# A relational graph layer: ScalarE fetches 27 chunks of source rows instead of 23, ahead of normalising raw rows, and SyncE fetches one chunk more

## The chip, the cores and the metric

The kernel runs on one core of a Trainium2 chip. The metric is device time in microseconds (us). Before the change three runs gave 2043.67 us in the median (2040.7 to 2045.21). Engines are called PE (matrix products), DVE (VectorE), ACT (ScalarE), POOL (GpSimd) and SP (SyncE).

## The reference, cut to what matters

```python
# N = 12500 nodes, D = 256; 212500 edges sorted by dst; 8 relations
h   = relu(layernorm(x))                       # [N, D]
hx  = einsum('ni,rio->rno', h, weight)         # per relation
agg = segment_sum(hx[edge_type, src], dst, N)  # over the edges
out = x + agg*sqrt(0.5) + h_bias + (h @ loop_weight)*sqrt(0.5)
```

The kernel turns the order round: for each node and relation it first sums the rows of h over the edges, and then multiplies these sums by the relation's weights.

## The kernel before

**First phase, to about 115 us.** All rows of x are normalised and written to `h_table` in DRAM, 1 KB a row: 256 fp16 values and 256 fp16 remainders. Meanwhile POOL gathers the first 96 "raw" chunks from x itself, since these need no table.

**Main loop.** The edges are cut into 1661 chunks of 128. A step s (98 of them) takes 17 chunks, k = 0 to 16 (the last step has 12). A chunk needs its 128 source rows in SBUF, one row for each partition. They come in four ways:

- the last chunk (k = 16) of steps 0 to 95 is raw and was gathered in the first phase; it is normalised later, 8 chunks at a time (`scale_raw`, L477): for group g DVE takes the statistics at k = 1 to 8 of step 8g-4 and then works out the scales behind k = 9 (`scales`, L622), for which it waits for ACT's square root (`deviation`, L441; DVE waits on `s_std` at L626); ACT then scales the rows;
- 36 chunks (k = 8 of steps 3, 6, 8, 11, 14, 16, ...) are fetched by SP, row by row, into three buffers (L315 to L327): registers are loaded with 32 row offsets at a time (L321), then 32 DMAs of 1 KB follow (L326);
- 23 chunks (k = 4 of steps 7, 11, 15, ...) are fetched by ACT in the same manner, 32 rows in each of its iterations (L509 to L520), into two buffers;
- the other 1506 chunks are gathered by POOL, one indirect DMA each (L400), into 15 buffers. Before every fourth gather it waits until the chunk 12 gathers back has been summed (L398).

PE multiplies the chunk's rows with a one-hot matrix (L991; L973 for raw chunks) into one of six PSUM banks, and before the end of each chunk it waits until DVE has added the chunk five back (L959). DVE adds the result into a ring of sums in SBUF (L787) and makes the one-hot matrix of the chunk one step on (L726). From k = 5 on PE also does the fp32 products of the tile two steps back (L921, then L926), 18 of them, spread over the chunks left in the step. After the last chunk come the products of the last two tiles (L914).

**ACT's iteration t** (L559 to L570) runs beside step t+2: it stores the result of tile t-1 once DVE has it (DVE does so behind k = 1), clears a ring slot, copies the transposed own rows, issues two loads, normalises a raw group in every eighth iteration, and fetches 32 rows. Every engine runs its own instructions in order, and waits are semaphores written by hand.

Of the kernel before, what the change touches and what calls it, by code (L numbers as in the profile page):

```python
# [4 lines left out]
def relational_graph_layer(nc, x, src, dst, etype, weight, h_bias, loop_weight, out, edge_chunks):  # L5
# [8 lines left out]
    P = 128  # L14
    N, D = x.shape
    R = weight.shape[0]
    C = dst.shape[1]
    E_CHUNKS = edge_chunks
    TILES = -(-N // P)
    STEPS = TILES  # L20
    K = C // STEPS
# [8 lines left out]
    NB = 15  # L30
    SB = 3
    AB = 2
# [18 lines left out]
    SYNC_K = K // 2  # L51
    SYNC_STEPS = [range(3, STEPS - 1, 8), range(6, STEPS - 1, 8), range(8, STEPS - 1, 8)]
    SCALAR_K = 4
    SCALAR_STEPS = range(7, STEPS - 1, 4)
    SCALAR_ROWS = [(0, 32), (32, 64), (64, 96), (96, 128)]
    SYNC_LOAD = 32
    ROW_BYTES = 4 * D

# [15 lines left out]
    table_bytes = table.rearrange("n d -> (n d)").bitcast(mybir.dt.uint8).rearrange("(a b) -> a b", a=1)  # L74

    sync_steps = sorted(s for steps in SYNC_STEPS for s in steps)
    sync_chunks = [K * s + SYNC_K for s in sync_steps]
    list_ranges = [(K * steps[0] + SYNC_K, K * steps.step, len(steps)) for steps in SYNC_STEPS]
    scalar_chunks = [K * s + SCALAR_K for s in SCALAR_STEPS]
    list_ranges.append((K * SCALAR_STEPS[0] + SCALAR_K, K * SCALAR_STEPS.step, len(SCALAR_STEPS)))  # L80
    listed = [a + d * i for a, d, n in list_ranges for i in range(n)]
    LISTED = len(listed)

# [1 line left out]
    with ctx:  # L85
        def sb(name, shape, dt):
            return ctx.enter_context(nc.sbuf_tensor(name, shape, dt))
# [4 lines left out]
        def sem(name):  # L92
            return ctx.enter_context(nc.semaphore(name))
# [21 lines left out]
        rows = sb("rows", [P, NB + SB + AB, 2 * D], fp16)  # L115
        list_low = sb("list_low", [P, LISTED], i32)
        list_parts = sb("list_parts", [P, 2, LISTED], fp16)
        row_offsets = sb("row_offsets", [LISTED, P], i32)
# [100 lines left out]
        scalar_landed = [sem(f"scalar_rows_landed{b}") for b in range(AB)]  # L219
# [4 lines left out]
        summed = sem("chunk_summed")  # L224
# [56 lines left out]
        def raw_step(s):  # L281
            if s == 0:
                return 0
            g = (s + 4) // G
            return g if (s + 4) % G == 0 and 0 < g < RAW_GROUPS else None
# [5 lines left out]
        def _(sp):  # L291
# [23 lines left out]
            def fetch_rows(j):  # L315
                b = j % SB
                if j >= SB:
                    sp.wait_ge(summed, sync_chunks[j - SB] + 1)
                q = listed.index(sync_chunks[j])
                for p in range(0, P, SYNC_LOAD):  # L320
                    _, start = nc.values_load_multi_w_load_instructions(  # L321
                        row_offsets[q:q + 1, p:p + SYNC_LOAD], engines=[mybir.EngineType.SP],
                        min_val=0, max_val=(N - 1) * ROW_BYTES,
                        skip_runtime_bounds_check_because="the sources of edges are nodes")
                    for i in range(SYNC_LOAD):
                        sp.dma_start(rows[p + i:p + i + 1, NB + b, :].bitcast(mybir.dt.uint8),  # L326
                                     table_bytes[:, bass.ds(start[i], ROW_BYTES)]).then_inc(sync_landed[b], 16)  # L327
# [112 lines left out]
        def _(act):  # L440
# [15 lines left out]
            for i in range(LN_GROUPS + 1):  # L456
                n, g = group_rows(i)
                b = i % 2
# [18 lines left out]
            def scale_raw(g):  # L477
                i = LN_GROUPS + 1 + g
                deviation(i)
                act.wait_ge(s_scale, i + 1)  # L480
                act.wait_ge(s_raw[g], 16 * G)
                for j in range(G):
                    last = nc.scalar.activation(raw[:, G * g + j, :], raw[:, G * g + j, :], ACT.Relu,  # L483
                                                bias=shift[:, i % 2, j:j + 1], scale=rstd[:, i % 2, j:j + 1])
                last.then_inc(s_norm, 1)

            def clear_tile(t):
                act.wait_ge(out_ready, t + 1)
                nc.scalar.copy(ring[:, :, ring_slot(t):ring_slot(t) + P],  # L489
                               zeros[:, :].unsqueeze(1).broadcast_to([P, HR, P])).then_inc(cleared, 1)  # L490

            def own_tile(t):
                n = P if t < TILES - 1 else LAST
                if t >= 2:
                    act.wait_ge(hT_ready, t - 1)
                act.dma_start(own[0:n, t % 2, :], table[t * P:t * P + n, :]).then_inc(own_landed[t % 2], 16)

            def own_x_tile(t):
                n = P if t < TILES - 1 else LAST
                if t >= 2:  # L500
                    act.wait_ge(scaled, t - 1)
                act.dma_start(own_x[0:n, t % 2, :], x[t * P:t * P + n, :]).then_inc(x_landed[t % 2], 16)

            def store_tile(t):
                n = P if t < TILES - 1 else LAST
                act.wait_ge(result_ready, t + 1)
                act.dma_start(out[t * P:t * P + n, :], result[0:n, t % 2, :]).then_inc(stored[t % 2], 16)

            def fetch_rows(t):  # L509
                j, (a, b) = t // len(SCALAR_ROWS), SCALAR_ROWS[t % len(SCALAR_ROWS)]  # L510
                if a == 0 and j >= AB:
                    act.wait_ge(summed, scalar_chunks[j - AB] + 1)
                q = listed.index(scalar_chunks[j])
                _, start = nc.values_load_multi_w_load_instructions(
                    row_offsets[q:q + 1, a:b], engines=[mybir.EngineType.Activation],
                    min_val=0, max_val=(N - 1) * ROW_BYTES,
                    skip_runtime_bounds_check_because="the sources of edges are nodes")
                for p in range(a, b):
                    act.dma_start(rows[p:p + 1, NB + SB + j % AB, :].bitcast(mybir.dt.uint8),
                                  table_bytes[:, bass.ds(start[p - a], ROW_BYTES)]).then_inc(scalar_landed[j % AB], 16)  # L520

            def copy_hT(t, to=own_hT):
                act.wait_ge(hT_ready, t + 1)
                nc.scalar.copy(to[:, :, :], ps_hT[:, 0:D].rearrange("p (h n) -> p h n", h=H)  # L524
                               ).then_inc(hT_copied, 1)
# [21 lines left out]
            with act.If(unfit < 1):  # L547
                for b in range(2):
                    act.wait_ge(s_tab[b], TAB_DONE[b])
                act.wait_ge(s_split, LN_GROUPS + 1)  # L550
                for a, b in ((0, 2 * P), (2 * P, SPAN)):
                    nc.scalar.copy(ring[:, :, a:b], zeros[:, 0:1].unsqueeze(1).broadcast_to([P, HR, b - a])
                                   ).then_inc(s_zeros, 1)
                for t in range(2):
                    own_tile(t)
                own_x_tile(0)
                scale_raw(0)
                act.wait_ge(list_ready, 1)
                for t in range(TILES - 2):  # L559
                    if t >= 1:  # L560
                        store_tile(t - 1)
                        if t <= TILES - RING + 1:
                            clear_tile(t - 1)
                    copy_hT(t)
                    own_tile(t + 2)
                    own_x_tile(t + 1)
                    if raw_step(t + 2) is not None:
                        scale_raw(raw_step(t + 2))
                    if t < len(SCALAR_ROWS) * len(scalar_chunks):
                        fetch_rows(t)  # L570
                for i in range(2):
                    copy_hT(TILES - 2 + i, last_hT[i])
                store_tile(TILES - 3)
                own_x_tile(TILES - 1)
                for i in range(2):
                    store_tile(TILES - 2 + i)
# [517 lines left out]
```

## Time and profile before

| | |
|---|---|
| median of three runs | 2043.67 us |
| the profiled execution's own time | 2044.47 us |
| its span | 2042.7 us |
| POOL busy | 1522.1 us, 75% |
| PE busy | 1529.7 us, 75% |
| DVE busy | 1335.0 us, 65% |
| ACT busy | 342.8 us, 17% |
| 16 DMA engines, share in the main loop | 0.46 |
| granted TensorE clock, mean | 0.878 |

The busy figures don't count instructions that issue DMAs or load registers. ACT's 17% is therefore its arithmetic alone, and SP, which only issues, has no busy time at all. For these two the time between rows is what counts.

### The profile page before, as it was taken

What the parts mean: (1) busy time and instruction counts of PE and PEld (TensorE: products, weight loads), DVE (VectorE), ACT (ScalarE), POOL (GpSimd) and SP (SyncE); (2) the same over time, 40 slices, a digit from 0 to 9 for tenths busy, and PEclk for the clock granted to TensorE, in tenths of its full rate; (3) what the DMA queues carried; (4) which work ended last, traced back from release to release, by engine and by line L of the source; (5) the groups of instructions that cost most, each with busy time, mean ns of one, the idle gap of its engine ahead of it and who ended that gap; (6) DMA issues with size and microseconds to landing.
All of it is one profiled execution on the core that took longest, in us unless ns stands there. A gap on an engine that the chain in (4) does not pass through costs nothing.

```text
span 2042.7 us, 45665 instructions
## 1 busy us (share of the span) xinstructions
PE 1529.7 (75%) x10568; PEld 1179.3 (58%) x10568; DVE 1335.0 (65%) x4141; ACT 342.8 (17%) x427; POOL 1522.1 (75%) x1610
## 2 busy tenths in 40 slices
PE   0027788788887887888877878878778878878878
PEld 0015566566666665666666656656666666656656
DVE  7856666666766666666666666666666666666662
ACT  5640111111111111111110210210210210210110
POOL 7777777777777777777777777777777777777773
PEclk9997888888888889888989889888888889888888
DMA  9964444444444444444444444444444444444442
GB/s 357 340 226 122 125 134 134 125 133 134 126 133 131 129 134 128 131 134 127 131 134 127 133 133 126 134 133 125 134 134 126 133 133 127 134 130 129 134 129 70
DMA packets 141489, 290.71 MB, mean 142 GB/s; under 512 B 38542, under 2 KB 86026, under 8 KB 138142
## 3 DMA queue, kind: packets, MB, share of 16 engines
q0 software_dynamic: 76896, 210.08, 35.8%
q10 hardware_dynamic: 49922, 54.25, 8.1%
q1 hardware_dynamic: 14396, 23.45, 3.7%
q8 instruction: 84, 1.38, 0.3%
q14 instruction: 191, 1.56, 0.2%
HBM read 262.02 MB, written 25.60 MB: 141 GB/s over the span
## 4 chain that ended last, share of the span: by engine, by line
POOL 38%; PE 24%; DMA 22%; issue 13%; DVE 1%; ACT 1%; POOLq 0%; SPq 0%; ACTq 0%; DVEq 0%
POOL rows L400 38%; DMA rows<-h_table,src_i 18%; PE psum L921 16%; PE psum L991 7%; DMA h_table<-room 4%; PE psum L914 1%; ACT psum L466 1%; DMA room<-x 1%; PE psum L926 0%; DVE stats L602 0%; PE psum L890 0%; PE psum L973 0%; DVE mv L609 0%; PE psum L905 0%; POOLq L85 0%
## 5 line engine op out<-in xcount | busy, mean ns | idle before, releaser
L400 POOL DMA_INDIRECT rows<-h_table,src_i x1506 | 1428.1, 948 | 461.7 <-issue 423.3
L787 DVE TENSOR_TENSOR room<-room,psum 128x256 f32 x1661 | 696.5, 419 | 582.0 <-PE psum L991 493.8
L921 PE MATMUL psum<-w_sb,room 128*128 128x256 f32 x3072 | 1001.6, 444 | 0.0
L991 PE MATMUL psum<-onehot,rows 128*128 128x128 f16 x6260 | 674.4, 238 | 388.7 <-DMA rows<-h_table,src_i 384.4
L991 PEld LDWEIGHTS psum<-onehot,rows 128*128 128x128 f16 x6260 | 480.0, 106 | 682.5 <-DMA rows<-h_table,src_i 509.8
L921 PEld LDWEIGHTS psum<-w_sb,room 128*128 128x128 f32 x3072 | 591.2, 219 | 49.1
L726 DVE TENSOR_SCALAR onehot<-lane,base_i 128x128 f16<-128x128 f16 x1565 | 434.0, 278 | 64.1
L489 ACT COPY room<-zeros 128x2048 f32<-128x2048 f32 x94 | 178.5, 1899 | 1459.9 <-DVE result L754 1212.6
L926 PE MATMUL psum<-w_sb,own_hT 128*128 128x256 f32 x384 | 119.7, 394 | 0.0
L389 POOL DMA_INDIRECT raw<-x,src_i x96 | 93.0, 969 | 31.1 <-issue 28.9
L1035 PE MATMUL psum<-unfit_p,ones 128*1 128x4 f32 x2 | 0.2, 166 | 114.4 <-DVE room L644 114.4
L1035 PEld LDWEIGHTS psum<-unfit_p,ones 128*1 128x1 f32 x2 | 0.1, 80 | 114.4 <-issue 114.4
L973 PEld LDWEIGHTS psum<-raw_onehot,raw 128*128 128x128 f32 x384 | 58.6, 194 | 6.8 <-ACT raw L483 2.0
L973 PE MATMUL psum<-raw_onehot,raw 128*128 128x128 f32 x384 | 59.5, 278 | 1.7 <-ACT raw L483 1.7
L926 PEld LDWEIGHTS psum<-w_sb,own_hT 128*128 128x128 f32 x384 | 58.2, 191 | 0.1
L483 ACT ACTIVATE raw<-raw,shift,rstd 128x256 f32<-128x256 f32 x96 | 48.5, 587 | 16.4 <-DVE shift L637 16.4
L751 DVE SCALAR_TENSOR_TENSOR result<-psum,own_x 128x256 f32<-128x256 f32 x98 | 40.8, 417 | 14.2 <-PE psum L914 13.8
L890 PE MATMUL psum<-ident,own 128*128 128x128 f16 x392 | 49.8, 265 | 0.0
L466 ACT ACTIVATE psum<-room,shift,rstd 128x256 f32<-128x256 f32 (+1 forms) x98 | 49.0, 553 | 3.7 <-DVE shift L637 3.6
L754 DVE TENSOR_TENSOR result<-result,bias_b 128x256 f32<-128x256 f32 x98 | 42.0, 428 | 3.3
L524 ACT COPY own_hT<-psum 128x256 f32<-128x256 f32 x96 | 35.2, 367 | 41.7 <-PE psum L890 41.5
L602 DVE BATCH_NORM_STATS2 stats<-room 128x6 f32<-128x256 f32 (+1 forms) x98 | 33.3, 412 | 13.5 <-DMA room<-x 13.4
(57 smaller groups left out, 276.1 us busy)
## 6 DMA issues: line engine op xcount, KB each, us to landing
rows<-h_table SPq DMA_DIRECT2D x4608, 1.0 KB
rows<-h_table ACTq DMA_DIRECT2D x2944, 1.0 KB
rows<-h_table,src_i POOLq DMA_INDIRECT x1506
own<-h_table ACTq DMA_DIRECT2D x97, 128.0 KB
own_x<-x ACTq DMA_DIRECT2D x97, 128.0 KB
out<-result ACTq DMA_DIRECT2D x97, 128.0 KB
room<-x SPq DMA_DIRECT2D x12, 1024.0 KB, 7.9
h_table<-room ACTq DMA_DIRECT2D x12, 1024.0 KB, 8.5
```

The source lines that it names most:

```text
L389: nc.gpsimd.indirect_dma_start(out=raw[:, r, :], out_offset=None, in_=x[:, :], in_offset=bass.IndirectOffsetOnAxis(ap=src_i[:, c:c + 1], a ...
L400: nc.gpsimd.indirect_dma_start(out=rows[:, q % NB, :], out_offset=None, in_=table[:, :], in_offset=bass.IndirectOffsetOnAxis(ap=src_i[:, c ...
L466: last = nc.scalar.activation(hp[0:n, b, j, :], xg[0:n, i % XB, j, :], ACT.Relu, bias=shift[0:n, b, j:j + 1], scale=rstd[0:n, b, j:j + 1])
L483: last = nc.scalar.activation(raw[:, G * g + j, :], raw[:, G * g + j, :], ACT.Relu, bias=shift[:, i % 2, j:j + 1], scale=rstd[:, i % 2, j: ...
L489: nc.scalar.copy(ring[:, :, ring_slot(t):ring_slot(t) + P], zeros[:, :].unsqueeze(1).broadcast_to([P, HR, P])).then_inc(cleared, 1)
L726: nc.vector.tensor_scalar(onehot[:, c % K, :], lane[:, :], slot[:, c:c + 1], None, ALU.is_equal).then_inc(onehot_ready, 1)
L787: nc.vector.tensor_tensor(window, window, sum_of(c).rearrange("p (a w) -> p a w", w=W), ALU.add).then_inc(added, 1)
L890: last = nc.tensor.matmul(ps_hT[:, h * P:(h + 1) * P], own[:, b, part * D + h * P:part * D + (h + 1) * P], ident[:, :], start=(part == 0), ...
L921: nc.tensor.matmul(ps_out[:, 0:D], nodes[:, m, :], w_sb[:, h, r, :], start=(m == 0), stop=False)
L926: last = nc.tensor.matmul(ps_out[:, 0:D], own_hT[:, h, :], w_sb[:, h, R, :], start=False, stop=(h == H - 1))
L973: last = nc.tensor.matmul(sum_of(c)[:, h * P:(h + 1) * P], raw[:, s, h * P:(h + 1) * P], raw_onehot[:, :], start=True, stop=True)
L991: last = nc.tensor.matmul(sum_of(c)[:, h * P:(h + 1) * P], now[:, part * D + h * P:part * D + (h + 1) * P], onehot[:, k, :], start=(part = ...
```

## The change

ACT fetches 27 chunks instead of 23, at k = 4 of steps 7, 10, 13, 17, 20, 23, ... to 93. The 27 x 128 = 3456 rows are dealt out evenly at 192/5 = 38.4 rows an iteration, that is 38 or 39, which ends in the 90th iteration (before: 92 iterations with 32). A register load still takes 32 offsets at most, and a fetch does not run over the end of a chunk in one load, so each iteration has two loads. The fetch now stands ahead of `scale_raw`, where it stood behind it. SP fetches a 37th chunk, number 1659, which is k = 10 of the last step. POOL gathers 1501 chunks instead of 1506. The list of the fetched chunks is 64 long instead of 59 and is set up by three more pieces on DVE before the loop.

```diff
-    SCALAR_STEPS = range(7, STEPS - 1, 4)
-    SCALAR_ROWS = [(0, 32), (32, 64), (64, 96), (96, 128)]
+    SCALAR_STEPS = [range(7, STEPS - 1, 10), range(10, STEPS - 1, 10), range(13, STEPS - 1, 10)]
+    SCALAR_ROWS, SCALAR_TILES = 192, 5
...
-    sync_chunks = [K * s + SYNC_K for s in sync_steps]
+    sync_chunks = [K * s + SYNC_K for s in sync_steps] + [E_CHUNKS - 2]
...
+    list_ranges.append((E_CHUNKS - 2, 1, 1))
...
             def fetch_rows(t):
-                j, (a, b) = t // len(SCALAR_ROWS), SCALAR_ROWS[t % len(SCALAR_ROWS)]
-                if a == 0 and j >= AB:
-                    act.wait_ge(summed, scalar_chunks[j - AB] + 1)
-                q = listed.index(scalar_chunks[j])
-                _, start = nc.values_load_multi_w_load_instructions(
...
+                first = t * SCALAR_ROWS // SCALAR_TILES
+                end = min((t + 1) * SCALAR_ROWS // SCALAR_TILES, P * len(scalar_chunks))
+                while first < end:
+                    j, a = first // P, first % P
+                    b = min(P, a + end - first, a + SYNC_LOAD)
+                    if a == 0 and j >= AB:
+                        act.wait_ge(summed, scalar_chunks[j - AB] + 1)
+                    q = listed.index(scalar_chunks[j])
+                    _, start = nc.values_load_multi_w_load_instructions(
...
+                    first += b - a
...
                     own_x_tile(t + 1)
+                    fetch_rows(t)
                     if raw_step(t + 2) is not None:
                         scale_raw(raw_step(t + 2))
-                    if t < len(SCALAR_ROWS) * len(scalar_chunks):
-                        fetch_rows(t)
```

On ACT, in the iteration t = 2, the first that normalises raw rows inside the loop. Before (L514 and L519 are the register load and the row DMAs):

```order
L507 DMA out<-result 128x256 [waits result_ready]
L489 COPY room<-zeros 128x16x128 [waits out_ready]
L524 COPY own_hT<-psum 128x256 [waits hT_ready]
L496 DMA own<-h_table 128x512 [waits hT_ready]
L502 DMA own_x<-x 128x256 [waits product_scaled]
L446 ACTIVATE std<-mv,eps 128x8 [waits scale_ready,variance_ready]
L483 ACTIVATE raw<-raw,shift,rstd 128x256 [waits raw_rows_landed1,scale_ready]
L483 ACTIVATE raw<-raw,shift,rstd 128x256 x7
L514 TENSOR_LOAD row_offsets
L519 DMA rows<-h_table 1x1024 x32
```

The same iteration now, with the line numbers of the changed kernel (L520 and L525 are the register load and the row DMAs, L448 the square root):

```order
L509 DMA out<-result 128x256 [waits result_ready]
L491 COPY room<-zeros 128x16x128 [waits out_ready]
L532 COPY own_hT<-psum 128x256 [waits hT_ready]
L498 DMA own<-h_table 128x512 [waits hT_ready]
L504 DMA own_x<-x 128x256 [waits product_scaled]
L520 TENSOR_LOAD row_offsets
L525 DMA rows<-h_table 1x1024 x32
L520 TENSOR_LOAD row_offsets
L525 DMA rows<-h_table 1x1024 x7
L448 ACTIVATE std<-mv,eps 128x8 [waits scale_ready,variance_ready]
L485 ACTIVATE raw<-raw,shift,rstd 128x256 [waits raw_rows_landed1,scale_ready]
L485 ACTIVATE raw<-raw,shift,rstd 128x256 x7
```

The square root, which DVE waits for, moved behind 2 loads and 39 row DMAs; a second load and 7 rows are new.

On SP, the end of its fetches. Before, the last rows of the 36th chunk and the wait for the end of the program:

```order
L321 TENSOR_LOAD row_offsets
L326 DMA rows<-h_table 1x1024 x32
L321 TENSOR_LOAD row_offsets
L326 DMA rows<-h_table 1x1024 x32
L348 UNCONDITIONAL_BRANCH [waits result_stored1,result_stored0]
```

The same place now (L323 and L328 are the register load and the row DMAs):

```order
L323 TENSOR_LOAD row_offsets
L328 DMA rows<-h_table 1x1024 x32
L323 TENSOR_LOAD row_offsets [waits chunk_summed]
L328 DMA rows<-h_table 1x1024 x32
L323 TENSOR_LOAD row_offsets
L328 DMA rows<-h_table 1x1024 x32
L323 TENSOR_LOAD row_offsets
L328 DMA rows<-h_table 1x1024 x32
L323 TENSOR_LOAD row_offsets
L328 DMA rows<-h_table 1x1024 x32
L350 UNCONDITIONAL_BRANCH [waits result_stored1,result_stored0]
```

A whole chunk of four loads and 128 row DMAs stands behind the 36th, and its first load waits until the chunk three fetches back (k = 8 of step 91) has been summed.

## Rows read from the trace of the kernel before

**Rows 1.** Section 1 of the page: busy time, share of the span, instructions.
```profile
PE 1529.7 (75%) x10568; PEld 1179.3 (58%) x10568; DVE 1335.0 (65%) x4141; ACT 342.8 (17%) x427; POOL 1522.1 (75%) x1610
```

**Rows 2.** Waits: engine, line, released by: us in total, times, longest us.
```profile
POOL rows L400 <- issue: 423.3, 1380, 2.5
PE psum L991 <- DMA rows<-h_table,src_i: 384.4, 470, 15.8
...
POOL rows L400 <- PE psum L991: 35.4, 116, 0.3
```

**Rows 3.** Line L400: shortest/median/longest in ns, first and last start in us.
```profile
L400 POOL DMA_INDIRECT rows<-h_table,src_i x1506: 941/947/1197, 128.2 to 2014.6; - x189
```

**Rows 4.** Windows: stretch; busy of PE, PEld, DVE, ACT, POOL; clock; DMA share; GB/s.
```profile
1050.00:1250.00 200.00, 161.72 (x1142) 123.26 (x1141) 132.01 (x404) 26.06 (x29) 151.30 (x160) 0.90 0.46 131
...
2010.40:2016.00 5.60, 5.60 (x23) 4.64 (x24) 0.84 (x2) 0.37 (x1) 3.95 (x5) 0.54 0.38 114
```

**Rows 5.** Timeline of ACT, two iterations: start, duration, line, idle before.
```profile
986.35 0.38 ACTq L507 DMA_DIRECT2D out<-result  x1
...
997.71 0.30 ACT L446 ACTIVATE std<-mv,eps 128x8 f32<-128x8 f32 x1 [8.76 <-DVE mv L609]
...
1012.56 0.38 ACTq L507 DMA_DIRECT2D out<-result  x1
...
1016.33 10.61 ACTq L519 DMA_DIRECT2D rows<-h_table  x32
1026.99 0.38 ACTq L507 DMA_DIRECT2D out<-result  x1
```

**Rows 6.** Register loads by line: shortest/median/longest ns, first and last start.
```profile
L514 ACTq TENSOR_LOAD <-row_offsets x92: 1996/2203/2295, 176.8 to 1932.9; - x92
...
L347 SPq TENSOR_LOAD <-unfit_i x1: 485/485/485, 130.6 to 130.6; - x1
...
L546 ACTq TENSOR_LOAD <-unfit_i x1: 1124/1124/1124, 116.3 to 116.3; - x1
...
L775 DVEq TENSOR_LOAD <-offsets x488: 316/346/715, 127.0 to 2017.3; - x163
```

**Rows 7.** Timeline of DVE around the scales of one raw group.
```profile
999.12 0.17 DVE L637 SCALAR_TENSOR_TENSOR shift<-mv,rstd 128x8 f32<-128x8 f32 x1
...
1005.70 0.41 DVE L787 TENSOR_TENSOR room<-room,psum 128x256 f32 x1
...
1006.77 0.42 DVE L754 TENSOR_TENSOR result<-result,bias_b 128x256 f32<-128x256 f32 x1
1007.11 0.41 DVE L787 TENSOR_TENSOR room<-room,psum 128x256 f32 x1
...
1007.73 0.41 DVE L787 TENSOR_TENSOR room<-room,psum 128x256 f32 x1
...
1008.68 0.42 DVE L787 TENSOR_TENSOR room<-room,psum 128x256 f32 x1 [0.25 <-issue]
```

**Rows 8.** Timeline of PE: k = 15 of that step.
```profile
1001.70 0.39 PE L991 MATMUL psum<-onehot,rows 128*128 128x128 f16 x4
```

**Rows 9.** Line L326 on SP: its row DMAs.
```profile
L326 SPq DMA_DIRECT2D rows<-h_table x4608: 219/220/438, 133.5 to 1953.4; - x192
```

**Rows 10.** Timeline of POOL in the last step: gathers for k = 5 and 11.
```profile
2006.99 1.07 POOL L400 DMA_INDIRECT rows<-h_table,src_i  x1 [0.30 <-issue]
...
2014.62 0.95 POOL L400 DMA_INDIRECT rows<-h_table,src_i  x1 [0.30 <-issue]
```

**Rows 11.** Timeline of PE in the last step.
```profile
2010.39 0.61 PE L991 MATMUL psum<-onehot,rows 128*128 128x128 f16 x4 [1.36 <-DMA rows<-h_table,src_i]
2010.80 2.87 PE L921 MATMUL psum<-w_sb,room 128*128 128x256 f32 x6
...
2018.32 1.51 PE L921 MATMUL psum<-w_sb,room 128*128 128x256 f32 x6
...
2020.81 0.39 PE L991 MATMUL psum<-onehot,rows 128*128 128x128 f16 x4
```

More of the change, by code:

```diff
@@ L76, in relational_graph_layer @@
     sync_steps = sorted(s for steps in SYNC_STEPS for s in steps)
-    sync_chunks = [K * s + SYNC_K for s in sync_steps]
+    sync_chunks = [K * s + SYNC_K for s in sync_steps] + [E_CHUNKS - 2]
     list_ranges = [(K * steps[0] + SYNC_K, K * steps.step, len(steps)) for steps in SYNC_STEPS]
-    scalar_chunks = [K * s + SCALAR_K for s in SCALAR_STEPS]
-    list_ranges.append((K * SCALAR_STEPS[0] + SCALAR_K, K * SCALAR_STEPS.step, len(SCALAR_STEPS)))
+    scalar_steps = sorted(s for steps in SCALAR_STEPS for s in steps)
+    scalar_chunks = [K * s + SCALAR_K for s in scalar_steps]
+    list_ranges += [(K * steps[0] + SCALAR_K, K * steps.step, len(steps)) for steps in SCALAR_STEPS]
+    list_ranges.append((E_CHUNKS - 2, 1, 1))
     listed = [a + d * i for a, d, n in list_ranges for i in range(n)]
@@ L509, in fetch_rows @@
             def fetch_rows(t):
-                j, (a, b) = t // len(SCALAR_ROWS), SCALAR_ROWS[t % len(SCALAR_ROWS)]
-                if a == 0 and j >= AB:
-                    act.wait_ge(summed, scalar_chunks[j - AB] + 1)
-                q = listed.index(scalar_chunks[j])
-                _, start = nc.values_load_multi_w_load_instructions(
[L515 to L520, printed above, removed]
+                first = t * SCALAR_ROWS // SCALAR_TILES
[7 more added lines that the diff above has]
+                    _, start = nc.values_load_multi_w_load_instructions(
+                        row_offsets[q:q + 1, a:b], engines=[mybir.EngineType.Activation],
+                        min_val=0, max_val=(N - 1) * ROW_BYTES,
+                        skip_runtime_bounds_check_because="the sources of edges are nodes")
+                    for p in range(a, b):
+                        act.dma_start(rows[p:p + 1, NB + SB + j % AB, :].bitcast(mybir.dt.uint8),
+                                      table_bytes[:, bass.ds(start[p - a], ROW_BYTES)]
+                                      ).then_inc(scalar_landed[j % AB], 16)
+                    first += b - a
             def copy_hT(t, to=own_hT):
```

## The prediction

> **What bounds the kernel now.** I read the busy shares first, then the waits, then POOL's line, then ACT's timeline. The shares alone decide nothing: PE and POOL are both at 75% [rows 1]. The waits do. POOL's idle time before its gathers is put down to "issue", 1380 times, and where PE is named it is never more than 0.3 us, the same gap as always, so POOL never really waits for a buffer. PE does wait for gathered rows, 384 us in all [rows 2]. POOL runs from 128.2 to 2014.6 us without a break [rows 3]: (2014.6 - 128.2)/1505 = 1.253 us a gather, 0.95 of it busy. Its row of 160 gathers in 200 us says the same [rows 4]. So POOL's number of gathers sets the time, until the last step.
>
> There it ends before the last gather. PE gets k = 5 at 2010.39, 3.4 us after that gather's start at 2006.99. After that PE has three products for each chunk and falls behind: it comes to k = 10 at 2020.81, while the gather of k = 11, POOL's last, starts at 2014.62 [rows 10, 11]. So the chain is: gathers up to k = 5 of the last step, then PE alone.
>
> **The change part by part.**
>
> *Gathers removed.* Of the five, four are ACT's new chunks, all ahead of k = 5 of the last step: 4 x 1.253 = 5.0 us. The fifth is k = 10 of that step, where PE is some 7 us behind POOL, so it is worth 0. If PE were not behind it would be worth 1.25; both ends stay in the range.
>
> *ACT's iteration.* An iteration without any wait is the one from 1012.56 to 1026.99: 14.43 us, with one load and 32 rows [rows 5]. A row costs 10.61/32 = 0.33 us (its duration there), so 6.4 more cost 2.1 us. A second load is added in each iteration. A load of 32 offsets takes 2.20 us; one of a single word took 0.49 on SP and 1.12 on ACT (once, at the start), and DVE's loads of up to four words take 0.35 [rows 6]. So a load of 6 or 7 words lies between 0.35 and 2.2 us. I take the line from SP's one word to 32 words, 0.055 us a word: 0.43 fixed and 6.4 words, 0.8 us. ACT's iteration becomes 14.43 + 2.1 + 0.8 = 17.3 us, with ends of 16.9 and 18.7. The step that it must keep up with: ten steps have 170 chunks, less 10 raw, 3.75 of SP and 3 of ACT, 153.25 gathers or 192.1 us, 19.2 us a step. ACT has 1.9 us in hand for each.
>
> *The square root behind the fetch.* In a raw iteration ACT now waits no more for DVE; DVE waits for ACT. Before, the iteration began at 986.35 and the square root came at 997.71, after 8.76 us of ACT idling [rows 5]. Now it comes 17.3 us after the start, at 1003.7: 6 us late, and DVE stands there behind k = 9. Behind DVE stand its adds. PE goes on for the six PSUM banks and stops at the end of k = 15, which it had at 1001.70 [rows 8]. It is let go when DVE has done the chain from the square root to the shift (997.71 to 999.29, 1.6 us [rows 5, 7]) and the add of k = 10: 1003.7 + 2.0 = 1005.7, 3.6 us late. POOL had issued gather (1001.7 - 128.2)/1.253 = 697 by then. Counting chunks, k = 15 of this step (44) is gather 693, and POOL first stops before gather 707, for the sum of 695: at 1014.4. PE is past that by about 1008. So POOL does not stop, with some 6 us to spare, and the stall costs nothing. 11 such iterations times nothing is nothing.
>
> *What is late next.* DVE then has nine adds to catch up before the result of the tile: 0.62 us from one to the next, or 0.95 where it loads offsets (three times), 6.0 us in all, then 1.5 to the end of the result [rows 7]. ACT's next iteration starts with storing that result, so a raw iteration lasts 17.3 + 1.6 + 6.0 + 1.5 = 26.4 us, 7.2 more than a step. The seven plain ones after it give back 7 x 1.9 = 13. ACT is even again after four of them. A lag of 7 us meanwhile does no harm: PE needs the copied own rows some 13 us after ACT normally has them, and the fetched chunks are used two steps (38 us) after the iteration that ends them.
>
> *SP's 37th chunk.* SP takes (1953.4 - 133.5)/36 = 50.6 us a chunk without a wait [rows 9]. The 37th would be issued by 2004 and landed by about 2007. PE, 5 us earlier than before, needs it at 2020.8 - 5.0 = 2015.8 [rows 11]. Hidden, with 9 us to spare; if SP were slower by more than 0.5% it would not be.
>
> *The longer list* costs DVE a few small operations ahead of the loop, beside POOL, which starts on its own: 0.
>
> *A rule weighed.* The DMA engines' share in the loop is 0.46 and POOL's pitch is the issue of gathers [rows 4]. The Trainium skill ("DMA: Bandwidth & Descriptors", section "Issuing engines are not separate DMA queues") says that all issuing engines end on the same 16 DMA engines, and that spreading DMAs over them only saves sequencer time, usually small. By this rule the change would give nothing. The trace agrees with its first half, but here the sequencer's time is just what bounds. The same page ("Latency and other measured facts") gives a register load a floor of about 600 ns; DVE's 346 ns lie under it, and with it the second load would cost much what I take.
>
> **The sum.** Profiled execution 2044.5 - 5.0 + 0 = 2039.5. The median of the runs shown is 0.8 below the profiled time: 2038.7 us.
>
> **The rivals.**
>
> *ACT's loop becomes the bound (slower).* Eight iterations are 8T + 9.1, where T is the plain iteration, against eight steps of 153.7. They part at T = 18.1, that is with a second load of 1.6 us. For it: if a load costs 2.2 us whatever its length, T is 18.7; ACT's own one-word load took 1.12. Against it: SP's single word and DVE's four took a quarter of the 32 words' time or less [rows 6]. Its price: at T = 18.7 each raw group leaves 5 us more of lag; from about 6 us of lag POOL stops at each of them. Ten periods: 50 - 6 = 44 us, less the 5: 2083 us. At T = 18.3 it would be 2051.
>
> *The 37th chunk lands late.* If ACT's extra rows make SP's DMAs 1% slower, it is 18 us later, PE waits 9, and the end is 2043.7 - 5 + 9 = 2048. Near 0.6% it just eats the gain. For it: SP has no idle time to catch up with. Against it: the wait for its slot is long over by then, and its pitch has been even for 36 chunks.
>
> *No change, 2043.* By the bound of the DMA engines (share 0.46 speaks against it), or because the tail gives it back: in the last step PE had a granted clock of 0.54 from k = 5 to 2016 us, almost all at the lower of its two levels, 1.2 GHz [rows 4]. Six product matmuls took 2.87 us there against 1.51 later [rows 11], some 2.5 us in two chunks. Where such a stretch falls can differ with the new alignment: twice as long it takes half of the gain, without it 2.5 us more are won.
>
> *The fifth gather counts too:* 2037.4 us. It needs PE to be ahead of POOL at the end, which [rows 10, 11] deny.
>
> **How the numbers follow.** A difference of 0.2% (4.1 us) is about what can be told from none, so faster means under 2039.6; the forecast is just beyond it. Forecast case 64%, with a range of its own from 2035.5 to 2041.5 by the tail's clock; two thirds of it count as faster. Fifth gather 8%, all faster. No change 10%. SP late 7%, half of it slower. ACT's loop 11%, nearly all slower. That gives faster 0.53, same 0.31, slower 0.16. The range is 2035.5 to 2046.0.
>
> **What would show it.** L400's successor has 1501 gathers, still 1.253 us apart, with no long idle time named for PE. ACT's plain iterations behind a raw one are 17.3 us apart, the short register loads take 0.5 to 1 us, and the ACT square root has no idle time for DVE before it while DVE's reciprocal waits about 6 us for ACT. After each raw group ACT waits for DVE's result again by the fifth iteration. PE doesn't wait for k = 10 of the last step. The prediction is wrong if plain iterations are over 18.1 us, if POOL has idle time of microseconds at steps 12, 20, ..., or if its pitch has grown.

## The result, and the profile after

The changed kernel takes 2279.08 us (median of 4 runs, 2278.1 to 2280.64), the kernel before 2042.18 in the same comparison (4 runs, 2040.67 to 2045.21): 1.116 times as long, interval 1.1142 to 1.1177. The prediction, 2038.7 us and at most 2046.0, was wrong by 240 us and in its sign. The profiled execution took 2279.28 us, with a span of 2277.5.

The page of the kernel after, sections 1 and 4 (busy shares against [rows 1], then the chain of work that ended last, by engine and line):
```profile
PE 1447.1 (64%) x10568; PEld 1163.9 (51%) x10568; DVE 1287.3 (57%) x4147; ACT 342.2 (15%) x427; POOL 1515.3 (67%) x1605
...
ACTq 17%; issue 8%; PE 5%; POOL 1%; DVE 1%; DMA 1%; ACT 1%; POOLq 0%; DVEq 0%
ACTq L525 13%; ACTq L520 3%; PE psum L928 2%; POOL rows L402 1%; PE psum L998 1%; DMA rows<-h_table,src_i 1%; PE psum L921 1%; ACTq L504 1%; PE psum L933 1%; ACT room L491 1%; DVE room L794 0%; ACTq L509 0%; PE psum L980 0%; DVE onehot L733 0%; DVE result L758 0%
```
POOL's work is what it was (1515 against 1522 us), in a span 235 us longer: it is the waiting that grew. The chain, in which ACT's queue had 0% before, is now led by it: L525 is its row DMAs, L520 its register loads (L519 and L514 before). The shares add up to 34%, since the profile follows this chain back only as far as 1516 us.

The waits of the kernel after, against [rows 2]:
```profile
ACT room L491 <- issue: 1433.7, 76, 22.3
...
PEld psum L998 <- DVE room L794: 284.5, 31, 27.7
POOL rows L402 <- PE psum L998: 282.9, 131, 23.4
...
PE psum L933 <- ACT own_hT L532: 275.6, 57, 8.9
DVE mv L638 <- ACT std L448: 268.9, 11, 27.0
```
Read them from POOL backwards. POOL waits 282.9 us for PE, up to 23.4 at once, where it never waited over 0.3 us; PE waits for DVE's adds; DVE waits for ACT's square root, 11 times, 27 us at most; and ACT waits for nobody ("issue"): it is busy with its own row DMAs and loads.

Line L402 of the kernel after (ns shortest/median/longest, first and last start), against [rows 3]:
```profile
L402 POOL DMA_INDIRECT rows<-h_table,src_i x1501: 940/946/1204, 128.7 to 2249.4; - x188
```
Five gathers fewer, each as long as before, yet the last begins 234.8 us later, just what the span grew by. 27 of the intervals between gathers are over 1.6 us, and what they have above POOL's usual pitch adds up to 242 us.

One raw iteration of ACT in the kernel after, that is one which also normalises a group of raw rows, with the four before it (start, duration, line, idle before), against [rows 5]:
```profile
1017.10 0.38 ACTq L509 DMA_DIRECT2D out<-result  x1
...
1040.89 0.38 ACTq L509 DMA_DIRECT2D out<-result  x1
...
1041.96 0.44 ACTq L504 DMA_DIRECT2D own_x<-x  x1
1049.85 15.11 ACTq L525 DMA_DIRECT2D rows<-h_table  x39
1065.00 0.38 ACTq L509 DMA_DIRECT2D out<-result  x1
...
1065.98 0.49 ACTq L504 DMA_DIRECT2D own_x<-x  x1
1068.76 14.30 ACTq L525 DMA_DIRECT2D rows<-h_table  x38
1083.10 0.38 ACTq L509 DMA_DIRECT2D out<-result  x1
...
1106.30 0.38 ACTq L509 DMA_DIRECT2D out<-result  x1
...
1124.74 0.30 ACT L448 ACTIVATE std<-mv,eps 128x8 f32<-128x8 f32 x1 [15.85 <-issue]
...
1133.97 0.37 ACTq L509 DMA_DIRECT2D out<-result  x1
```
From store to store the iterations take 23.8, 24.1, 18.1, 23.2 and, raw, 27.7 us. All five have 38 or 39 rows. The long ones differ from the 18.1 one in the gap between the own_x DMA and the rows, 7.4 us at 1042 against 2.3 at 1066: the register load. DVE and POOL at that raw step:
```profile
1125.13 0.17 DVE L638 TENSOR_SCALAR mv<-mv 128x8 f32<-128x8 f32 x1 [25.50 <-ACT std L448]
```
```profile
1127.23 0.94 POOL L402 DMA_INDIRECT rows<-h_table,src_i  x1 [20.72 <-PE psum L998]
```
The loads as a whole, and the two of the gaps above alone (all of L520, then the windows 1041 to 1050 and 1066 to 1069), against [rows 6]:
```profile
L520 ACTq TENSOR_LOAD <-row_offsets x180: 1055/2067/7382, 177.2 to 2166.4; - x180
...
L520 ACTq TENSOR_LOAD <-row_offsets x1: 7333/7333/7333, 1042.4 to 1042.4; - x1
...
L520 ACTq TENSOR_LOAD <-row_offsets x1: 2157/2157/2157, 1066.5 to 1066.5; - x1
```
I sorted all 180 by how many offsets they load and by whether the first one's place in the list is a multiple of 4 (offsets are words of 4 bytes). Medians of the trace's durations, in us:
```
words         6      7      12     13     25     26     32
multiple      1.06   1.29   1.09   -      2.06   -      2.20
other         1.67   1.89   -      3.05   -      5.97   7.31
```
Of the 36 loads of 32 words that start elsewhere none is under 7.10 us, of the 36 that start on a multiple none over 2.32, and the short ones don't overlap either. Before, all 92 started at 0, 32, 64 or 96. An iteration's loads come to 6.2 us on average, 3.4 where both start on multiples.

### The profile page after: what moved, and what is told of

It is laid out like the page before. It is cut to its first block and busy times, and to the rows that moved or that the text cites. A ratio compares the mean times of both kernels' runs of the same rounds, so it can differ in the third digit from the quotient of the medians.

```text
span 2277.5 us, 47038 instructions
## 1 busy us (share of the span) xinstructions
PE 1447.1 (64%) x10568; PEld 1163.9 (51%) x10568; DVE 1287.3 (57%) x4147; ACT 342.2 (15%) x427; POOL 1515.3 (67%) x1605
## 5 line engine op out<-in xcount | busy, mean ns | idle before, releaser
L402 POOL DMA_INDIRECT rows<-h_table,src_i x1501 | 1421.0, 947 | 703.2 <-issue 418.5
L928 PE MATMUL psum<-w_sb,room 128*128 128x256 f32 x3072 | 889.3, 403 | 50.6 <-DVE result L758 49.8
L998 PE MATMUL psum<-onehot,rows 128*128 128x128 f16 x6260 | 612.0, 235 | 379.3 <-DVE room L794 278.5
L998 PEld LDWEIGHTS psum<-onehot,rows 128*128 128x128 f16 x6260 | 487.3, 106 | 594.2 <-DVE room L794 284.5
L928 PEld LDWEIGHTS psum<-w_sb,room 128*128 128x128 f32 x3072 | 517.2, 193 | 94.5 <-DVE result L758 49.7
L933 PE MATMUL psum<-w_sb,own_hT 128*128 128x256 f32 x384 | 178.8, 561 | 275.7 <-ACT own_hT L532 275.6
L933 PEld LDWEIGHTS psum<-w_sb,own_hT 128*128 128x128 f32 x384 | 83.7, 269 | 285.8 <-ACT own_hT L532 285.8
L980 PEld LDWEIGHTS psum<-raw_onehot,raw 128*128 128x128 f32 x384 | 86.8, 279 | 13.3 <-ACT raw L485 1.6
L980 PE MATMUL psum<-raw_onehot,raw 128*128 128x128 f32 x384 | 86.1, 368 | 1.4 <-ACT raw L485 1.4
L897 PE MATMUL psum<-ident,own 128*128 128x128 f16 x392 | 44.5, 245 | 0.0
```

The costliest lines, as they stand in the source:

```text
L402: nc.gpsimd.indirect_dma_start(out=rows[:, q % NB, :], out_offset=None, in_=table[:, :], in_offset=bass.IndirectOffsetOnAxis(ap=src_i[:, c ...
L928: nc.tensor.matmul(ps_out[:, 0:D], nodes[:, m, :], w_sb[:, h, r, :], start=(m == 0), stop=False)
L933: last = nc.tensor.matmul(ps_out[:, 0:D], own_hT[:, h, :], w_sb[:, h, R, :], start=False, stop=(h == H - 1))
L980: last = nc.tensor.matmul(sum_of(c)[:, h * P:(h + 1) * P], raw[:, s, h * P:(h + 1) * P], raw_onehot[:, :], start=True, stop=True)
L998: last = nc.tensor.matmul(sum_of(c)[:, h * P:(h + 1) * P], now[:, part * D + h * P:part * D + (h + 1) * P], onehot[:, k, :], start=(part = ...
```

## The experiments

The kernels are lettered by the comparison that they shared. In f and h the kernel before took its usual 2042 us. In e, j, k and m it took 2998 to 3044 us; there SP's queue leads the chain of every kernel profiled, with 51 to 58% of the span, so the times answer little of what was asked, and mostly durations are used.

### e: alignment, the 37th chunk, shifted loads (kernel before at 3043.88)

e1_aligned is the kernel after, with each iteration's rows cut at multiples of 4:
```
-                first = t * SCALAR_ROWS // SCALAR_TILES
-                end = min((t + 1) * SCALAR_ROWS // SCALAR_TILES, P * len(scalar_chunks))
+                first = t * SCALAR_ROWS // SCALAR_TILES // 4 * 4
+                end = min((t + 1) * SCALAR_ROWS // SCALAR_TILES // 4 * 4, P * len(scalar_chunks))
```


> The changed kernel with one difference: the shares of rows begin and end at multiples of four rows (36 or 40 an iteration instead of 38 or 39; 38.4 in the mean as before, 27 chunks, fetch ahead of normalising, SP's 37th chunk kept). Theory A (a register load on ACT that starts off a multiple of four words is read word by word, 0.21 us each; the loads alone made ACT's loop the bound): first loads 2.2 us instead of up to 7.4, the two loads of an iteration 2.9 us instead of 6.2, a plain iteration of ACT 14.8 + 2.9 = 17.7 us, eight iterations 8 x 17.7 + 9.2 = 150.8 against 153.7 of POOL: 2038 us, 5 below before. Rival B (the loads were slow because they run beside ACT's own copies and more row DMAs, whatever their start): loads as long as in the changed kernel, 2270 us. Rival C (loads are cured but DVE's wait for the square root holds POOL all the same): 5 to 8 us of POOL idle at each of 11 raw groups, 2090 to 2130 us.

e3_sp37 is the kernel before with SP's 37th chunk alone (`+ [E_CHUNKS - 2]` and its list entry).

> The kernel before with one difference: SP fetches chunk 1659 (k = 10 of the last step) as its 37th. Theory A: PE is behind POOL in the last step, so one gather less there gives nothing: within 1 us of before, ratio 0.9995 to 1.0005. Rival B: the end hangs on POOL's last gather, 1.25 us less (ratio 0.9994). Rival C: SP's chunk lands after PE comes to it, 1 to 10 us more.

e4_shift1 is the kernel before with a copy of the list for ACT that starts one word off a multiple of 4; e4_shift4 has `4:4 + P` in place of `1:1 + P`.
```
+        act_room = sb("act_room", [LISTED, P + 4], i32)
+        act_offsets = act_room[:, 1:1 + P]
-                    row_offsets[q:q + 1, a:b], engines=[mybir.EngineType.Activation],
+                    act_offsets[q:q + 1, a:b], engines=[mybir.EngineType.Activation],
```


> The kernel before (23 chunks, 32 rows an iteration, one load, fetch behind normalising) with ACT's offsets in a copy of their own that lies one word further in each partition, so that every load of ACT starts one word behind a multiple of four. Nothing else differs but one small operation on DVE ahead of the loop. Theory A (start of the load): each load 7.2 us instead of 2.2, plain iteration 14.6 + 5.0 = 19.6 against a step of 19.3, a raw one 31; eight are 7 x 19.6 + 31 = 168 against 154, so 14 us for each of 11 groups less what the buffers take up: 2160 to 2200 us. Rival B (length, second load or more rows are to blame, not the start): 2042 us.

> Control of the one-word shift: the same copy, but four words further, so that loads start at a multiple of four words again. Theory A: loads 2.2 us, 2042 us. Rival (a separate copy or its place slows the loads): as slow as with one word.

Measured: e1 3062.9 us (ratio 1.0062, 1.004 to 1.0085), e3 3073.26 (1.0093, 1.0073 to 1.0113), e4_shift1 3027.74 (0.9945, 0.9922 to 0.9968), e4_shift4 3047.27 (one run). The chain of e3_sp37 shows what bound them, SP's row DMAs and loads:
```profile
SPq 57%; issue 34%; DVE 2%; DMA 2%; PE 2%; another core or an unknown queue 2%; ACT 1%; DVEq 0%; ACTq 0%
```
Its line L327 has row DMAs of up to 1474 ns at the issuing engine, where [rows 9] have 438 at most. The loads still answer their question. Line L516 in e4_shift1 and in e4_shift4:
```profile
L516 ACTq TENSOR_LOAD <-act_room x92: 5517/7122/7365, 275.4 to 2878.3; - x92
```
```profile
L516 ACTq TENSOR_LOAD <-act_room x92: 802/2184/2282, 274.4 to 2900.1; - x92
```
The same 32 words from the same copy cost 7.12 us from one word off and 2.18 from four words off. Nothing else differs between the two kernels, so it is the start that counts, not the copy or the length.

### f1_aligned: what the alignment cost

The kernel of e1_aligned again.

> The changed kernel with shares of rows that begin and end at multiples of four rows, run again, since in the comparison before this one the kernel before itself took 3044 us, with SP's row DMAs as the bound, so that ACT could not decide the time. If the kernel before takes its usual 2042 us: theory A (start of the loads alone made ACT's loop the bound): loads of 1.1 to 2.2 us, plain iteration of ACT 17.7 us, eight iterations 150.8 against POOL's 153.7, 2038 us. Rival C (loads are cured, but DVE's wait for the square root holds POOL all the same, 5 to 8 us at each of 11 raw groups): 2090 to 2130 us. If the kernel before is at 3044 again: no difference of theories can be seen in the time.

Measured: 2079.25 us (2078.52 to 2081.64), ratio 1.0181 (1.0167 to 1.0195), against 2041.75. 200 of the 237 us are gone with the alignment alone, but not the last 37. The loads and the waits of f1_aligned:
```profile
L520 ACTq TENSOR_LOAD <-row_offsets x180: 587/1504/2312, 175.8 to 1952.3; - x180
```
```profile
PE psum L998 <- DMA rows<-h_table,src_i: 333.7, 354, 14.6
...
DVE mv L638 <- ACT std L448: 96.8, 11, 11.6
POOL rows L402 <- PE psum L998: 83.2, 125, 5.4
```
ACT's plain iteration while it lags is 18.2 us, the raw one 27.6. POOL still stops behind raw steps, by some 5 us where it was 20. What its intervals between gathers have above the usual pitch adds up to 44.5 us, and five gathers fewer give 6.3 back. That leaves 38, about the 37 lost. The chain of f1_aligned has no part of SP in it:
```profile
DMA 28%; POOL 27%; PE 19%; issue 12%; ACTq 8%; DVE 4%; ACT 1%; DVEq 0%; POOLq 0%; SPq 0%
```

### f4_shift1: slow loads in the kernel before

The kernel of e4_shift1 again.

> The kernel before with every load of ACT starting one word behind a multiple of four, run again for the same reason. Theory A, on a chip where the kernel before takes 2042 us: loads 7.1 us, ACT's plain iteration 19.6, a raw one 31, 168 against 154 for eight, 2160 to 2200 us. Rival B (length, the second load or more rows are to blame): 2042 us.

Measured: 2089.49 us (2088.66 to 2090.31), ratio 1.0231 (1.0212 to 1.025). Its loads and waits:
```profile
L516 ACTq TENSOR_LOAD <-act_room x92: 6929/7162/7390, 176.5 to 1998.9; - x92
```
```profile
ACT room L491 <- issue: 1557.5, 91, 19.0
...
PE psum L930 <- ACT own_hT L526: 300.6, 72, 5.6
...
POOL rows L402 <- PE psum L995: 88.6, 131, 4.1
```
Slow loads alone, with nothing else of the change, cost 47 us. The plain iteration is 19.6 us as expected, but a raw one only 22.8 where some 31 were expected: with the fetch behind the raw scaling, as before, a lagging ACT finds DVE's variances ready. 7 x 19.64 + 22.75 = 160.2 us for eight steps against POOL's 153.7; 11 times these 6.5 us are 72. The 47 measured would be what is left once the lag has grown as far as POOL's lead allows; POOL's first stop comes only at 561 us, in the third group, but the lead itself was not measured.

### h: order, 37th chunk, alignment with the old order, split row DMAs

h3_order_only is the kernel before with these two lines moved:
```
+                    if t < len(SCALAR_ROWS) * len(scalar_chunks):
+                        fetch_rows(t)
                     if raw_step(t + 2) is not None:
                         scale_raw(raw_step(t + 2))
-                    if t < len(SCALAR_ROWS) * len(scalar_chunks):
-                        fetch_rows(t)
```


> The kernel before (23 chunks, 32 rows, one load an iteration, no 37th chunk) with the fetch ahead of normalising raw rows. Theory G: gathers complete at 4.1 us and ACT has 4.8 us in hand for each iteration, so DVE's hold (about 3.5 us late at the square root) does not stop POOL: within 1 us of before. Rival C (the order alone costs POOL some us at each of the 11 groups): 2060 to 2080 us.

Measured: 2041.11 us (2040.42 to 2043.58), ratio 0.9999 (0.999 to 1.0008). DVE does wait for the square root, and POOL doesn't notice. Waits of h3_order_only:
```profile
DVE mv L631 <- ACT std L446: 57.4, 11, 5.9
POOL rows L400 <- PE psum L991: 37.2, 122, 0.3
```
h4_sp37 is the kernel of e3_sp37.

> The kernel before with SP's 37th chunk as the only difference, once more, since in the first comparison SP's DMAs were slow in the kernel before too (3044 us). If before takes 2042 us: theory A (PE is behind POOL in the last step): ratio 0.9995 to 1.0005. Rival B (the end hangs on the last gather): ratio 0.9994. Rival C (the chunk is late): 1 to 10 us more.

Measured: 2043.53 us (2042.39 to 2044.5), ratio 1.0005 (0.9996 to 1.0014). SP's rows in it:
```profile
L327 SPq DMA_DIRECT2D rows<-h_table x4736: 219/220/558, 134.5 to 2005.1; - x198
```
h2_aligned_behind is f1_aligned with the fetch moved back behind the raw scaling.

> The aligned kernel with the fetch behind normalising raw rows again, as before the change; all else as aligned (2079 us). Theory G: POOL stops there because two things add up, gathers that complete 9 us late (which uses up its buffers) and DVE held 6 to 12 us by the fetch at each raw group. Without the hold POOL stops little: 2038 to 2046 us. Rival H: the late completions alone stop POOL: 2070 to 2080 us. Rival I: ACT becomes the bound, since a raw iteration is longer behind: over 2085.

Measured: 2087.64 us (2084.2 to 2090.93), ratio 1.023 (1.0216 to 1.0244). I had expected the old order to save what f1 still lost. It saved half of POOL's stops: they add up to 21 us instead of 44.5, and the last gather begins at 2029.4 instead of 2050.8. But the end came no sooner. Its SP line, PE's waits for fetched rows, and its chain near the end:
```profile
L328 SPq DMA_DIRECT2D rows<-h_table x4736: 219/220/572, 133.3 to 2057.1; - x198
```
```profile
PE psum L998 <- DMA rows<-h_table: 38.0, 9, 21.4
```
```profile
1900.92 1.17 ACTq L520
...
1938.74 17.95 DMA rows<-h_table
...
2045.06 2.23 SPq L323
2057.14 1.42 DMA rows<-h_table
```
Here the end hangs on SP's 37th chunk, which it finished issuing at 2057.1, 52 us later than in h4: PE's longest wait, 21.4 us, is for it. The 17.95 us at 1938.74 are the way of ACT's last row from issue to landing; PE stood idle for it for only 0.4 us.

h1_two_engines is f1_aligned with each fetched row sent as two parts of 512 B, to test whether a row's single DMA is what delays others:
```
-                                     table_bytes[:, bass.ds(start[i], ROW_BYTES)]).then_inc(sync_landed[b], 16)
+                                     table_bytes[:, bass.ds(start[i], ROW_BYTES)].rearrange("p (a b) -> p a b", a=2)).then_inc(sync_landed[b], 16)
```


> The aligned kernel (38.4 rows, shares at multiples of four, fetch ahead, 37th chunk) with each fetched row written in two pieces of 512 bytes to two places, so that one row DMA has two equal parts. In the aligned kernel 15 of the 16 completions of a gather come 2.4 to 2.8 us after its start, and the last one after 9.3 us (before: 4.1). Theory D: all row DMAs of SP and ACT, 4.5 a us, run on one DMA engine, which is nearly full; with two parts they run on two, the last completion comes back to under 4 us, POOL does not stop, 2038 us. Rival E: that engine's time goes by pieces and not by bytes, then two engines are as full as the one, last completion 9 us or more, 2079 us or slower. Rival F: the late completion has nothing to do with the row DMAs: unchanged 9 us, 2079.

Measured: 3938.16 us, ratio 1.9299 (1.9273 to 1.9325). No theory had this. SP's line:
```profile
L329 SPq DMA_DIRECT2D rows<-h_table x4736: 3/562/1436, 133.6 to 3915.1; - x198
```
A row DMA of two parts holds SP for 562 ns (median) instead of 220, a chunk takes 99 us instead of 49, and SP bounds the kernel. As the rows come at half the rate (2.3 a us), the test could not tell what it was for.

### What the completions show

The trace also records when each DMA's completions arrive; a gather has 16. Sorted by kernel (rate: SP's rows over the time from its first to its last, plus ACT's over that of its loads; then the 15th and the 16th completion after the gather's start, median of some 900 gathers in the main loop, and an SP chunk's issue of 128 rows, the mean):
```
                    rows/us  15th  16th us  SP chunk us  last SP row
before              4.21     2.77  4.11     48.1         1953.4
h4_sp37             4.21     2.79  4.11     48.1         2005.1
f4_shift1           4.15     2.78  3.83     48.1         1953.4
after               4.04     2.76  4.06     48.0         2190.7
f1_aligned          4.43     2.78  9.34     49.1         2042.1
h2_aligned_behind   4.42     2.78  9.67     49.5         2057.1
```
The 15th completion never changes. The last one comes 5 us later in just the two kernels that bring 4.4 rows/us, and only in these two do SP's own row DMAs take longer. The fetched rows are late there too: from the issue of a chunk's last row to its landing it takes 3.5 us on SP and 4.5 on ACT before, 10.4 and 11.2 in f1_aligned, 12.1 and 15.9 in h2_aligned_behind (medians).

That aligned loads alone don't do it, e1_aligned shows. It is the kernel of f1_aligned, but in its comparison, where SP issues slowly, it brings only 3.0 rows/us. Its fetched rows land 1.3 and 1.7 us after issue, and of the 1266 gathers in the main loop that have completions on record (few have all 16) none has one later than 5 us, where f1_aligned has them up to 13.3. So the lateness goes with the row rate. A run that varies the rate and nothing else was not obtained.

What the lateness costs is in part argued. Take SP first. From chunk to chunk it takes 50.6 us before, 51.7 in f1 and 52.1 in h2 (first rows of its first and its last chunk, their distance over the number of chunks between), so three chunks take 151.8, 155.0 and 156.3 us against the 153.7 of POOL's eight steps: SP had 1.9 us in hand for each eight steps, and the new rate takes more. Over 36 chunks it is 38 and 54 us, and SP's last row comes 37 and 52 us later than in h4. In h2 this sets the end.

In f1 it does not, near as the 37 us are to what f1 lost: SP has no part in its chain, and the loss is POOL's stops. These may come from the late completions, from ACT's loop, which is at its limit as well (7 x 18.2 + 27.6 = 155.0, some 14 us over 11 such periods), and from DVE's hold at the square root, 11.6 us at most; h2 without that hold has half of them. No run tells the first two apart.

### j, k, m: the rate and ACT's loop apart (kernel before at 3036, 2998 and 3004)

j1_35rows, k1_35rows and m1_35rows are one kernel: aligned loads, the old order, no 37th chunk, and 34.9 rows an iteration:
```
-    SCALAR_STEPS = [range(7, STEPS - 1, 10), range(10, STEPS - 1, 10), range(13, STEPS - 1, 10)]
-    SCALAR_ROWS, SCALAR_TILES = 192, 5
+    SCALAR_STEPS = [range(7, STEPS - 1, 11), range(11, STEPS - 1, 11), range(14, STEPS - 1, 11)]
+    SCALAR_ROWS, SCALAR_TILES = 384, 11
```


> Loads on multiples of 4, 25 ScalarE chunks (34.9 rows an iteration instead of 32 or 38.4), SP 36 chunks, fetch behind the raw scaling as before; 2 gathers fewer than before. Theory A (ScalarE's loop alone costs time): T about 15.9 us, so 8 steps of ScalarE take at most 138 to 141 us against POOL's 153.7, and the time is 2039 to 2041 (two gathers of 1.24 us less). Theory L (the rate of row DMAs is what costs: above some 4.2 rows/us a gather's last completion comes at 9 instead of 4 us and SP's own row DMAs grow from 226 to 233-237 ns, so that three SP chunks take 155-156 us against POOL's 153.7): at 2.53 + 34.9/19.2 = 4.35 rows/us the last completion lies between 4.1 and 9.3 us and SP's chunk between 48.1 and 49.1 us; time 2040 to 2055, with SP's 36th chunk ending at 1953 to 1990.

j2, k2 and m2_short_clear are f1_aligned with 8 of 128 columns cleared in each part. They leave out the rest of the clearing, so the sums start from old values:
```
-                nc.scalar.copy(ring[:, :, ring_slot(t):ring_slot(t) + P],
+                nc.scalar.copy(ring[:, :, ring_slot(t):ring_slot(t) + 8],
```


> f1_aligned (27 chunks, loads on multiples of 4, SP 37, fetch ahead) with ScalarE's clearing of the ring cut from 128 to 8 columns of each of the 16 parts, so the tiles' sums start from stale values: ScalarE's iteration is 1.5 us shorter, everything else as in f1. Theory A: T falls from 18.2 to 16.6, ScalarE's 8 steps from 155.0 to about 142, no stop of POOL: 2037 to 2041. Theory L: rows are issued at the same mean rate, the last completion stays at 9 us and SP's chunk at 49.1 us or more; SP's 37th chunk ends after 2035: 2065 to 2080.

j3_long_clear is h3_order_only with the clear in 22 pieces, j4_behind_no37 is h2_aligned_behind without the 37th chunk.

> h3_order_only (32 rows an iteration, fetch ahead of the raw scaling, 23 and 36 chunks) with ScalarE's clear done in 22 small pieces instead of one instruction, so that its iteration is some 3 to 5 us longer at the same row rate (T 17.5 to 19.5 instead of 14.4). Theory A: as in f1_aligned, 8T+9.4 against 153.7: about 2043 at T 18.0, 2060 to 2080 at T 18.2-18.7, 2110 at T 19.5. Theory L: the last completions stay at 4.1 us and SP's chunk at 48.1 us; only what 8T+9.4 exceeds 153.7 by costs, 11 times: 2043 to 2050 up to T 18.2, and above it 88 us per us of T.

> h2_aligned_behind without SP's 37th chunk (POOL gathers that chunk, 1 gather more). In h2 SP's 37th chunk ended at 2057, 52 us later than in h4, where the rows of ScalarE went at the old rate, and POOL's last gather began at 2029.2. Theory L (late SP ends h2's run): without the 37th the end follows POOL's last gather by 10.4 + 13.8 us: 2050 to 2062, 25 to 37 us less than h2's 2087.6. Theory A (ScalarE's loop set h2's time): 2085 to 2090, as h2.

The repeats had the same question: for k2_short_clear, 

> The kernel of j2_short_clear again, in a comparison where the kernel before hopefully takes its usual 2042 us (there it took 3036 and SP's chunks 77 us, which hides everything asked here). f1_aligned with the clear cut to 8 of 128 columns. Theory A (ScalarE's loop alone): T 16.6, 8 steps 142, time 2037 to 2041. Theory L (row rate): the gathers' last completion stays near 9 us, SP's chunk at 49.1 us or more, its 37th ends after 2035; 2065 to 2080.

and for m1_35rows, 

> The kernel of k1_35rows once more. Theory A: 2039 to 2041. Theory L: 4.35 rows/us, last completion between 4.1 and 9.3 us, SP's chunk between 48.1 and 49.1; 2040 to 2055, slower than before if three SP chunks take over 153.7 us.

Measured: j1 3028.64 (ratio 0.9987, 0.9961 to 1.0013), j2 3057.97 (1.0086, 1.0053 to 1.0119), j3 3054.43 (1.0068, 1.0044 to 1.0093), j4 3037.51 (1.0, 0.998 to 1.0019); k1 2998.44 (0.9992, 0.9963 to 1.0021), k2 3026.28 (1.0075, 1.004 to 1.011); m1 2996.06 (0.9968, 0.9935 to 1.0002), m2 3037.14 (1.0107, 1.0055 to 1.0158). SP's line in m1_35rows:
```profile
L327 SPq DMA_DIRECT2D rows<-h_table x4608: 2/220/1400, 211.7 to 2964.6; - x192
```
SP takes some 75 us to issue a chunk in all of them and bounds them: three are over 225 us, against POOL's 153.7. The kernels with a 37th SP chunk are slower by 0.6 to 1.1% and those without it the same, but for j3 (0.7%), whose cause I did not look for. None of this tells what ScalarE's loop costs from what the row rate costs at the usual pace, so that question stays open, and with it whether 34.9 rows beat the kernel before.

## Why the prediction was wrong

*Gathers removed: not refuted.* 1501 gathers at the old duration. What they save is not seen by itself, since no version with four fewer ran without other costs; the fifth alone (h4) was worth nothing, as forecast.

*ACT's iteration, the step that failed.* Forecast T = 17.3 us with ends of 16.9 and 18.7; measured 21.0 over the 78 plain iterations. Of the 3.7 us that are missing, 3.2 are loads: 6.2 us an iteration instead of 3.0. The forecast priced the second load (0.8 us; its aligned kin took 1.1 to 1.3, so that bound held) and left the first at 2.2 us. But the change also moves the start of both loads through the list, 38.4 rows at a time, and a load that starts off a multiple of 4 words costs 0.23 us a word (0.27 for 6 and 7 words). All 92 loads in [rows 6] start on multiples, so the row had only one of two prices in it; that the starts move was to be read in the diff. The remaining 0.5 us are rows: an iteration without its loads takes 14.8 us against 14.3 from [rows 5].

The rival "ACT's loop becomes the bound" is what happened, at 11%. Its own rule gives the size: it parts from POOL at T = 18.1, and 7 x 21.0 + 30.4 = 177.4 us against 153.7 for eight steps are 23.7 us, 11 times 261, less what the lag may grow before POOL stops (6 us as forecast, more at the start): measured 242. Its upper end, 2083 at T = 18.7, was far too low, because T was.

*The square root behind the fetch: right for an ACT that is on time, as forecast, and not for one that lags.* The raw iteration is T + 9.4 against T + 9.1. With ACT on time the stall is hidden, as forecast: h3_order_only loses nothing, and DVE's longest wait was 5.9 us where 6 were forecast. With a lagging ACT it isn't: DVE waits 27 us at most and POOL 19 to 23 at each raw group from the second on.

*SP's 37th chunk: right alone, wrong at the new rate.* Alone it is hidden (h4: 2005.1 against "by 2004"). The rival "lands late" assumed that ACT's extra rows slow SP by 1% or so, and gave it 7%. In the kernel after it played no part, since SP itself had to wait for a stopped PE. With the loads aligned SP's chunk is 2 to 3% longer, more than the rival assumed. In h2 that ends the kernel, in f1 it does not.

*No room for more rows.* The forecast took POOL as the only bound. f1_aligned and h2_aligned_behind show that without the slow loads the change would have cost 37 to 45 us instead of 237, and SP's margin of 1.9 us in 153.7 is a limit that [rows 9] had in them: 50.6 us a chunk, three chunks for every eight steps. It is the limit that h2 meets at its end; which one holds f1 back is open.

*A rule weighed.* With more of ACT's rows SP's chunk goes from 48.1 to 49.1 and 49.5 us, and POOL's gathers complete 5 us later. The Trainium skill ("DMA: Bandwidth & Descriptors", section "Issuing engines are not separate DMA queues") has all issuing engines end on the same 16 DMA engines, and this fits it. The prediction set the rule aside by the mean share of 0.46 in [rows 4]; a mean over 16 engines doesn't show whether a single one is near its limit. That one of them is, with 15 completions on time and the last one late, is a reading of the table; no run shows it.

## What to carry to other kernels

When a change moves where an instruction reads, check that the rows of the kernel before contain its new start: a price taken from aligned starts alone holds for those alone. Of a loop that must keep up with another, write down all the engines' margins per period, here 153.7 us against ACT's, SP's and POOL's own, before anything is added to one of them. And cut register loads from a list at multiples of 4 words: it took 200 us off this kernel.

## What the runs showed of the hardware

- A load of 32 words into ACT's registers takes 2.20 us when its first word stands on a multiple of 4 words (16 bytes) and 7.1 to 7.4 us otherwise; e4_shift1 and e4_shift4 differ in nothing else.
- Short aligned loads on ACT: 6 words 1.06 us, 7 words 1.29, 12 words 1.09, 25 words 2.06. DVE's took 0.35 for up to four words [rows 6].
- At 4.4 row DMAs/us the last of a gather's 16 completions comes at 9.3 to 9.7 us, at 4.0 to 4.2 at 3.8 to 4.1; the other 15 are in at 2.8 in every case. The kernel that has 9.3 at 4.4 rows/us had none recorded over 5 at 3.0 (f1_aligned, e1_aligned). Its fetched rows landed 10 to 11 us after issue at 4.4, 1.3 to 1.7 at 3.0.
- A row DMA in two parts of 512 B holds the issuing SP 562 ns instead of 220 (medians, h1_two_engines and f1_aligned).
- The same kernel took 2042 us in some comparisons and 2998 to 3044 in others, where the issue of a row DMA on SP took up to 1.5 us and SP bound it. Why is open.
